# A recommender's pair products on one core: three looked-up field pairs loaded in stages, gathers spread out, and ten accumulating DMAs

## The reference, cut to what matters

```
e = stack([tbl_f[ids[:, f]] for f in range(40)], axis=1)   # 512 samples, 40 fields, 64 numbers each
# z[b, p] = e[b, i] @ W[p] @ e[b, j] for each of the 780 pairs p = (i, j), i < j; W[p] is 64 x 64
h = concatenate([z, dense_ctx], axis=1)                    # 780 + 16 columns
h = relu(h @ W_top1 + b_top1)                              # 512 wide
h = relu(h @ W_top2 + b_top2)                              # 256 wide
y = h @ W_top3                                             # 1 wide
```

## Time and profile before

| | us |
|---|---|
| median of 3 runs (lowest, highest) | 331.17 (330.99, 332.05) |
| the profiled execution, its own time | 331.24 |
| its span in the trace | 329.4 |

### The profile page before, as it was taken

One profiled execution on the slowest core, in us unless ns is written; L12 is line 12 of the kernel. 1 busy time (PEld: TensorE's weight loads), 2 busy tenths in 40 slices (PEclk: granted clock), 3 DMA queues, 4 the chain that ended last, 5 costly groups with the idle time before them and its releaser, 6 DMA issues.

```text
span 329.4 us, 5579 instructions
## 1 busy us (share of the span) xinstructions
PE 309.2 (94%) x1480; PEld 109.2 (33%) x1480; DVE 250.0 (76%) x252; ACT 218.0 (66%) x1696; POOL 228.0 (69%) x192
## 2 busy tenths in 40 slices
PE   0599999999999999999999999999999999999997
PEld 0133342333333323333333333333333333334442
DVE  2296588786979797898899899989999987960000
ACT  1001120089947999399999999999999999810022
POOL 6777777777777777789848898898898463930000
PEclk9999999999999999999999999999999999999999
DMA  5843444343234249532322213322212200000000
GB/s 162 239 133 90 116 102 119 94 121 87 68 119 117 73 116 333 121 104 71 92 64 85 78 67 101 90 66 78 81 37 67 64 1 0 3 2 0 0 0 0
DMA packets 17866, 27.67 MB, mean 84 GB/s; under 512 B 4901, under 2 KB 5029, under 8 KB 17834
## 3 DMA queue, kind: packets, MB, share of 16 engines
q1 hardware_dynamic: 12074, 21.00, 21.6%
q0 software_dynamic: 4608, 4.73, 6.5%
q10 hardware_dynamic: 1152, 1.57, 1.7%
HBM read 22.57 MB, written 0.00 MB: 69 GB/s over the span
## 4 chain that ended last, share of the span: by engine, by line
PE 66%; POOL 19%; issue 8%; DVE 5%; DMA 2%; ACT 0%; DVEq 0%
PE ps_t L558 30%; POOL rows L342 14%; PE ps_z L580 13%; PE ps_t L541 11%; PE ps_t L589 5%; POOL wide_rows L342 5%; DVE prod L466 4%; PE ps_t L640 2%; PE ps_e L520 2%; PE ps_e L589 2%; DMA rows<-in_tbl,ids_sb 1%; DVE batched L480 1%; DMA ids_sb<-in_ids_t 1%; PE ps_t L645 1%; PE ps_t L618 0%
## 5 line engine op out<-in xcount | busy, mean ns | idle before, releaser
L386 ACT ACTIVATE batched<-batched 128x64 f32<-128x64 f32 x832 | 198.7, 247 | 0.0
L466 DVE TENSOR_TENSOR prod<-ps_t,E 128x1024 f32<-128x1024 f32 x148 | 171.0, 1216 | 21.6 <-PE ps_t L558 21.1
L386 ACT ACTIVATION_READ_ACCUMULATOR batched<-batched 128x1 f32 x832 | 160.7, 193 | 0.0
L558 PE MATMUL ps_t<-E,w_sb 64*128 64x512 f32 x592 | 145.0, 614 | 3.5 <-ACT E L370 1.3
L342 POOL DMA_INDIRECT rows<-in_tbl,ids_sb x128 | 121.3, 948 | 38.4 <-issue 38.3
L349 POOL TENSOR_TENSOR prod<-prod 128x1024 f32<-128x1024 f32 x38 | 88.8, 2374 | 18.6 <-DVE prod L466 18.5
L558 PEld LDWEIGHTS ps_t<-E,w_sb 64*128 64x128 f32 x592 | 51.0, 185 | 86.4 <-issue 56.0
L480 DVE TENSOR_TENSOR batched<-ps_t,wide_rows 128x1024 f32<-128x1024 f32 x52 | 60.0, 1217 | 8.4 <-PE ps_t L541 8.4
L370 ACT ACTIVATE E<-ps_e 128x512 f32<-128x512 f32 x18 | 10.7, 592 | 63.6 <-PE ps_e L520 41.2
L580 PE MATMUL ps_z<-prod,quads 128*32 128x512 f32 x360 | 52.4, 600 | 0.0
L541 PE MATMUL ps_t<-w_sb,E 64*128 64x512 f32 x208 | 48.2, 602 | 0.0
(11 more groups left out here) (39 smaller groups left out, 60.4 us busy)
## 6 DMA issues: line engine op xcount, KB each, us to landing
w_sb<-in_w_units SPq DMA_DIRECT2D x50, 256.0 KB, 2.7
E<-E SPq DMA_DIRECT2D x48, 64.0 KB, 2.0
rows<-in_tbl,ids_sb POOLq DMA_INDIRECT x128
w_sb<-in_w SPq DMA_DIRECT2D x7, 256.0 KB
E<-E ACTq DMA_DIRECT2D x24, 64.0 KB, 2.2
prod<-in_ids_by_field SPq DMA_DIRECT2D x2, 512.0 KB, 9.3
prod<-in_tbl SPq DMA_DIRECT2D x3, 312.5 KB
w_sb<-in_w SPq DMA_DIRECT2D x1, 512.0 KB
```

Of the source, the lines that this page charges most:

```text
L386: last = act.activation(products, products, ACT.Copy, accum_out=zt[:, b, at:at + 1])
L466: dve.tensor_tensor(prod[:, n % P_RING, s, :, :], ps_t[:, step % STEPS, :, :], multiplier, ALU.mult).then_inc(product_ready, 1)
L558: last = pe.matmul(ps_t[:, step % STEPS, j, :], w_sb[at:at + DIM, m % W_RING, col:col + P], E[at:at + DIM, slot_of(pairs_of(n)[s][j]), :], ...
```

## The change

A third pair, u = 2 (fields 34 and 35), is looked up too, with 16 products more; its eight gathers and four transposes go, and a third `turn_rows` comes. The transposes of u = 3 stand in the middle of the look-up of u = 2, and group 0 now waits for all four first pairs.

SP first loads the ids of fields 38 and 39 alone (4 KB). DVE casts them to float, PE spreads them over 128 partitions with two matmuls against `pick` (two rows, one of ones, one of zeros), and ACT copies the two results into `ids_wide`; the first broadcast DMA goes. SP waits for both tables of a pair before it issues the next pair's wide ids and tables, and for all six tables before the weights.

Gathers are issued one by one: each of a pair's eight has a due time, evenly spaced over the groups from the first group of the pair before to its own, less `GATHER_LEAD = 7`.

The halves of couples 7, 8, 10, 11 and 13 (groups 14 to 17, 20 to 23, 26 and 27) are added by DMAs with `accum_op=add`, 512 KB each, issued by POOL; PE waits for the DMA's semaphore and reduces with 8 instructions instead of 16.

The last product is made as four matmuls of 128 columns on four column blocks of the array (output rows 0, 32, 64, 96) instead of one of 512, and ACT's last copy is 97 x 128.

```
-FETCHED_AT = (0, 16)
-LOOKED_UP = 2
+FETCHED_AT = 8
+LOOKED_UP = 3
-GATHER_LEAD = 14
+GATHER_LEAD = 7
+DMA_COUPLES = (7, 8, 10, 11, 13)
+ADDED = ADDED_BY_POOL + ADDED_BY_DMA
+def gather_due(u, i):
+    first, last = first_group(u - 1), first_group(u)
+    return first + (i + 1) * (last - first) / (2 * BT) - GATHER_LEAD
-SPLIT_FIRST = (0, 2, 3, 1)
+SPLIT_FIRST = (0, 1, 3, 2)
-WIDE_AFTER = (1, 2)
+WIDE_AFTER = (0, 1, 2)
...
+            sp.dma_start(ids_first[:], ids_by_field[looked_up[0]:looked_up[0] + 2, :]).then_inc(ids_first_loaded, 16)
             sp.dma_start(ids_sb[:], ids).then_inc(ids_loaded, 16)
             for u in range(LOOKED_UP):
+                if u > 0:
+                    for f in looked_up[2 * u - 2:2 * u]:
+                        sp.wait_ge(small_loaded[f], 16)
+                    sp.dma_start(ids_wide[:, 2 * u:2 * u + 2, :].bitcast(I32),
...
+            for f in looked_up:
+                sp.wait_ge(small_loaded[f], 16)
             for m in range(W_RING):
                 load_weights(m)
...
             def add_halves(n):
                 pool.wait_ge(product_ready, FIRST_STEP["group", n] + 2)
+                if n in ADDED_BY_DMA:
+                    pool.dma_start(prod[:, n % P_RING, 0, :, :], prod[:, n % P_RING, 1, :, :],
+                                   accum_op=ALU.add).then_inc(halves_added_by_dma[n % P_RING], 16)
+                    return
...
+            gathers = [(u, i) for u in range(LOOKED_UP, KP) for i in range(2 * BT)]
             for n in range(NG):
-                while u < KP and first_group(u) <= n + GATHER_LEAD:
-                    gather(u)
-                    u += 1
+                while gathers and gather_due(*gathers[0]) <= n:
+                    gather(*gathers.pop(0))
...
+            for i in range(2):
+                act.wait_ge(ids_spread, i + 1)
+                act.activation(ids_wide[:, i, :], ps_t[:, 0, i, :], ACT.Copy).then_inc(ids_spread_copied, 1)
...
+            dve.tensor_copy(pick[:], ident[0:2, 0:2, None].to_broadcast([2, 2, P])).then_inc(pick_ready, 1)
+            dve.wait_ge(ids_first_loaded, 16)
+            dve.tensor_copy(ids_first_f[:], ids_first[:]).then_inc(ids_first_cast, 1)
...
+            for i in range(2):
+                pe.matmul(ps_t[:, 0, i, :], pick[:, i, :], ids_first_f[:], start=True, stop=True).then_inc(ids_spread, 1)
...
-                last = pe.matmul(y_bank[0:1, :], w3_sb[:, c:c + 1], h2[:, c, :],
-                                 start=(c == 0), stop=(c == H2 // P - 1))
+                for b in range(BT):
+                    last = pe.matmul(y_bank[32 * b:32 * b + 1, 0:P], w3_sb[:, c:c + 1], h2[:, c, b * P:(b + 1) * P],
+                                     start=(c == 0), stop=(c == H2 // P - 1))
```

More of the change, by code:

```diff
@@ L25 @@
 BLOCKS = 4
+LAST_Y = 32 * (BT - 1) + 1
 PER_CHUNK = 16
-FETCHED_AT = (0, 16)
-LOOKED_UP = 2
+FETCHED_AT = 8
+LOOKED_UP = 3
 CODE_RING = 7
@@ L80 @@
 ADDED_COUPLES = (14, 15, 16, 18, 19, 20, 21, 23, 24, 25, 26, 27, 28, 30, 31, 32, 33, 34, 35)
-ADDED = [n for n in range(NG) if n // 2 in ADDED_COUPLES]
+DMA_COUPLES = (7, 8, 10, 11, 13)
+ADDED_BY_POOL = [n for n in range(NG) if n // 2 in ADDED_COUPLES]
+ADDED_BY_DMA = [n for n in range(NG) if n // 2 in DMA_COUPLES]
+ADDED = ADDED_BY_POOL + ADDED_BY_DMA
 def arrival(k):
@@ L197, in tower_kernel @@
             "p (c n) -> p c n", c=CODE_RING)
+        at += CODE_RING * BATCH
+        ids_first = scratch[0:2, at:at + BATCH].bitcast(I32)
+        ids_first_f = scratch[0:2, at + BATCH:at + 2 * BATCH]
+        pick = scratch[0:2, at + 2 * BATCH:at + 2 * BATCH + 2 * P].rearrange("p (f n) -> p f n", f=2)
         z = sb("z", [P, ALL_CHUNKS, BATCH])
@@ L203, in tower_kernel @@
         b2_sb = sb("b2_sb", [P, H2 // P])
-        y_sb = sb("y_sb", [1, BATCH])
+        y_sb = sb("y_sb", [P, P])
         h1 = E[:, 0:H1 // P, :]
@@ L222, in tower_kernel @@
         wide_loaded = [sem(f"wide_loaded{u}") for u in range(LOOKED_UP)]
+        ids_first_loaded = sem("ids_first_loaded")
+        ids_first_cast = sem("ids_first_cast")
+        pick_ready = sem("pick_ready")
+        ids_spread = sem("ids_spread")
+        ids_spread_copied = sem("ids_spread_copied")
         small_loaded = {f: sem(f"small_loaded{f}") for f in looked_up}
@@ L242, in tower_kernel @@
         halves_added = sem("halves_added")
+        halves_added_by_dma = [sem(f"halves_added_by_dma{i}") for i in range(P_RING)]
         two_reduced = sem("two_reduced")
@@ L320, in _ @@
             sp.wait_ge(y_ready, 1)
-            sp.dma_start(out, y_sb[:]).then_inc(stored, 16)
+            sp.dma_start(out.rearrange("o (b n) -> (o b) n", b=BT), y_sb[0:LAST_Y:32, :]).then_inc(stored, 16)
             sp.wait_ge(stored, 16)
@@ L333, in _, with gather @@
             pool.wait_ge(ids_loaded, 16)
-            def gather(u):
-                k = KP - 1 - u
-                if u >= FIRST + G_RING:
+            def gather(u, i):
+                k, f, b = KP - 1 - u, i // BT, i % BT
+                if i == 0 and u >= FIRST + G_RING:
                     pool.wait_ge(transposed, u - G_RING - LOOKED_UP + 1)
[L339 to L345, removed]
+                col = (2 * k + f) * BT + b
+                pool.indirect_dma_start(
+                    rows_of(u, b)[:, f * DIM:(f + 1) * DIM], None, tables[2 * k + f],
+                    bass.IndirectOffsetOnAxis(ap=ids_sb[:, col:col + 1], axis=0),
+                ).then_inc(rows_semaphore(u), 16)
             def add_halves(n):
                 pool.wait_ge(product_ready, FIRST_STEP["group", n] + 2)
+                if n in ADDED_BY_DMA:
+                    pool.dma_start(prod[:, n % P_RING, 0, :, :], prod[:, n % P_RING, 1, :, :],
+                                   accum_op=ALU.add).then_inc(halves_added_by_dma[n % P_RING], 16)
+                    return
                 pool.tensor_tensor(prod[:, n % P_RING, 0, :, :], prod[:, n % P_RING, 0, :, :],
                                    prod[:, n % P_RING, 1, :, :], ALU.add).then_inc(halves_added, 1)
-            u = LOOKED_UP
+            gathers = [(u, i) for u in range(LOOKED_UP, KP) for i in range(2 * BT)]
             for n in range(NG):
-                while u < KP and first_group(u) <= n + GATHER_LEAD:
-                    gather(u)
-                    u += 1
+                while gathers and gather_due(*gathers[0]) <= n:
+                    gather(*gathers.pop(0))
                 if n in ADDED:
@@ L420, in _ @@
             act.wait_ge(y_summed, 1)
-            act.activation(y_sb[:], y_bank[0:1, :], ACT.Copy).then_inc(y_ready, 1)
+            act.activation(y_sb[0:LAST_Y, :], y_bank[0:LAST_Y, 0:P], ACT.Copy).then_inc(y_ready, 1)
         @block.vector
@@ L438, in encode @@
                 before = sum(len(codes_of) for codes_of in code_list[:u])
-                dve.wait_ge(wide_loaded[u], 16)
+                if u > 0:
+                    dve.wait_ge(wide_loaded[u], 16)
                 for j, (f, c) in enumerate(code_list[u], start=before):
@@ L443, in encode @@
                     used, i = splits[f][0], looked_up.index(f)
-                    dve.tensor_scalar(codes[0:used, j % CODE_RING, :], ids_wide[0:used, i, :], float(c),
+                    if u == 0 and c == 0:
+                        dve.wait_ge(ids_spread_copied, i + 1)
+                    wide = ids_wide[0:used, i, :] if u == 0 else ids_wide[0:used, i, :].bitcast(I32)
+                    dve.tensor_scalar(codes[0:used, j % CODE_RING, :], wide, float(c),
                                       first_row_f[0:used, i:i + 1], ALU.subtract, ALU.is_equal).then_inc(
@@ L502, in look_up_fields @@
                 for j, (f, c) in enumerate(code_list[u], start=before):
-                    if u == 1 and j - before in FETCHED_AT:
-                        transpose_fields(LOOKED_UP + FETCHED_AT.index(j - before))
+                    if u == LOOKED_UP - 1 and j - before == FETCHED_AT:
+                        transpose_fields(LOOKED_UP)
                     if c == 0:
@@ L567, in reduce_two @@
                     pe.wait_ge(product_ready, FIRST_STEP["group", g] + 2)
-                    if g in ADDED:
-                        pe.wait_ge(halves_added, ADDED.index(g) + 1)
+                    if g in ADDED_BY_POOL:
+                        pe.wait_ge(halves_added, ADDED_BY_POOL.index(g) + 1)
+                    elif g in ADDED_BY_DMA:
+                        pe.wait_ge(halves_added_by_dma[g % P_RING],
+                                   16 * sum(a % P_RING == g % P_RING for a in ADDED_BY_DMA if a <= g))
                 for s in range(2):
@@ L593, in _ @@
             pe.wait_ge(ident_ready, 1)
+            pe.wait_ge(pick_ready, 1)
+            pe.wait_ge(ids_first_cast, 1)
+            for i in range(2):
+                pe.matmul(ps_t[:, 0, i, :], pick[:, i, :], ids_first_f[:], start=True, stop=True).then_inc(ids_spread, 1)
             pe.wait_ge(sums_ready, 6)
```

8 lines of the change are left out of this document (4 added, 4 removed).

## The result

The changed kernel takes 329.3 us (median of 4, 329.06 to 329.45) against 331.36 before in the same comparison: ratio 0.9931, 95% interval 0.9919 to 0.9943. It is faster by 0.7% where 1.5% was forecast. The profiled execution's span is 327.5 us against 329.4.

| point | before | after | after - before |
|---|---|---|---|
| group 0 starts | 34.41 | 37.87 | +3.5 |
| transposes of u = 4 | 42.89 | 46.23 | +3.3 |
| transposes of u = 9 | 86.98 | 88.61 | +1.6 |
| batched unit 4 | 134.67 | 133.65 | -1.0 |
| turning of `zt` | 293.93 | 292.43 | -1.5 |

The account below looks back on a forecast made before the run. PE was taken as the bound, apart from table waits at the start and two waits for gathered rows. 331.24 + 0.8 - 1.6 - 3.5 - 0.8 = 326.1 us; likeliest case 323 to 329.5, range 322.4 to 331.5.

Parts of the forecast that it names:

- u = 4 is reached 0.8 later: Start: transposes of u = 4 come at 43.7 us, 0.8 later than before; 16 more products and SP's sleeping eat the gain.
- the third load round: Start: the third pair's ids and tables, issued at 18.6 us, land at 18.6 + 4.5 + 2.2 + 2.2 = 27.5.
- The first two rounds: Start: the second table lands at 9.1 us (8.3 to 10.3), the second pair's last table at 18.6.
- my central case: Start, likeliest course: PE does one product at 26.4 us, then waits until 27.5 for field 35.
- the Trainium skill's rule on the number of engines: Table loads: a DMA uses the largest number of engines up to 16 dividing its slowest dimension; 125 partitions give five.
- a PE wait before field 35: Start: a PE wait before field 34 or 35 was listed as a sign that the prediction is wrong.
- The pace of the first products: Start: pair 0's 19 products after the first take 9.4 us (8.2 to 10.3), ending at 18.5.
- Gathers: Pairs u = 8 and 9: with eight fewer POOL gathers, PE's waits for rows, 0.82 + 0.74, go: -1.6 us.
- Accumulates: Five couples' shorter reductions, 106 to 158 us: -3.5 us (2.9 to 4.3); each adding DMA takes 5.3, hidden.
- 5.7 free us cover 3.5: Accumulating couples: ACT's 5.7 us free from 106.9 to 160.3 us let it follow the 3.5 us gain.
- slow-accumulate rival: Reductions: adds at 8 us each keep the queue busy over 6.6 us, PE waits, total 340; chance 0.14.
- The end: Last product and ACT's copy: four 128-column products side by side and a shorter copy, -0.9 us, taken as -0.8.

Follow-up runs that it names:

- split tables: The changed kernel with each small table loaded by two DMAs, of 120 and 5 partitions, instead of one of 125: 326.9 us, ratio 0.9853.

## Why the prediction was wrong in size

*The failed step* is "u = 4 is reached 0.8 later" in the start, and in it the third load round, which lands the third pair at 27.5. Measured: 29.2, and u = 4 is 3.3 later. The first two rounds came as worked out (second table at 9.04, forecast 9.1; second pair at 18.6, forecast 18.6). The third took 10.6 us instead of 8.9: its broadcast 4.2 (4.5 taken), its two 250 KB tables together 6.4 instead of 2 x 2.2. This is no accident of one run: in all nine traces with these tables and waits the third round takes 10.5 to 11.0 us, the second, with more bytes, 9.2 to 10.0. The cause stays open. ACT's placing DMAs of pair 0 (issued from 20.93 to 23.45 us) run in the third round and not in the second, and with split tables, where ACT issues them only at the third round's end, the third is the shorter one; but they were never moved alone.

The products from field 35 on then took 7.8 us instead of 7.1: field 34's first product had run ahead of the wait, so the last one before the transposes stands alone on its half. 1.7 + 0.7 is the miss.

The waiting was the right mechanism, but my central case had it only by a hair (1.1 us). The run with split tables shows that the loads cost 2 us, and the Trainium skill's rule on the number of engines, cited in the prediction, was also the remedy. I used it to check a row instead of asking what it leaves waiting.

Two slips of the prediction belong here: the earlier trace rows has 16 GB/s, not 17, which changes nothing, and "a PE wait before field 35" is given as a sign of being wrong although the forecast itself has one.

*The pace of the first products* was mis-sized too: 9.4 us for 19 came out at 10.8, and pair 0 ended near 20 us instead of 18.5. It cost little, because it lay behind the same wait: without the accumulates it was 9.4, and field 35 still began at 29.1, after 1.71 us of waiting instead of 0.39. But with tables at 27.5, as forecast, PE would have come to field 35 at 28.8 in the changed kernel's trace. There the late tables alone cost 0.4 us; up to 1.7 when the pace is good.

*Gathers*, -1.6: right, 3.3 to 1.6 late is -1.7. What I had not seen is how much stood behind it: with two pairs PE waits for rows four times, 5.7 us in all, and 3.8 us for adds.

*Accumulates*, -3.5: measured 3.1 between the points of the ledger, 3.4 to 4.1 by taking them out. The landing time, 5.3 taken, was 5.8. ACT's "5.7 free us cover 3.5" was too kind: the sums bind from 138 to 168 us and take about 1 us back, as leaving sums out shows. The slow-accumulate rival did not come. With two more couples a slowdown did, but by way of the weights, not of the adds.

*The end*, -0.8: PE and ACT gave the 0.9, the store, which I had not priced, took 0.5 back; net -0.4.

Sum: +3.3 - 1.7 - 3.1 - 0.4 = -1.9 against +0.8 - 1.6 - 3.5 - 0.8 = -5.1.

## What to carry to other kernels

Where loads go out in rounds that wait for each other, each round's time is on the path as soon as the work between is shorter, so ask of each load how many DMA engines its slowest dimension lets it use: cutting 125 partitions into 120 and 5 took off 2.4 us, more than the whole change did (2.1). Work moved to another engine is worth its time only until the next engine binds; the windows of before name that engine (ACT 47.73 of 53.40 us, DVE 46.86). And DMAs moved into a stretch that is half full (a share of 0.60 before, from 100 to 135 us) can make a quite different transfer late.

## What the runs showed of the hardware that was not expected

- PE's products at the start run at half pace, though the granted clock reads 1.00 (the 2.4 GHz level), until a time that differs between traces whose start is the same code: 11.35 us without the accumulates, about 14.1 in the changed kernel. Before, where the first product starts at 10.70, it was 17.4.
- An accumulating DMA of 512 KB within SBUF costs POOL 1.02 us to issue and lands in 4.8 to 10.1 us, 5.8 in the median; with fourteen of them in 46 us beside the weights and gathers, the profile's DMA share reads 1.05, that is, full.
- A 2 KB store from four partitions took 2.05 us to the end of the span (2.0 to 2.1 in all fourteen traces with it), from one partition 1.54 (both traces).
